# The grouped projection stages of a one-core transformer kernel, spread over four engines

## The reference, cut to what matters

```python
x = x + _L3_attn_ref(_layernorm(x, axis=-1), ...)

def _L3_attn_ref(hidden, ...):                 # rmsnorm eps 1e-6, 16 query heads and 4 key heads of 8
    x = hidden
    x = x + global_latent_attn(rmsnorm(x, norm1_w), g_wq, g_kv_down, g_k_up, g_v_up, g_wo)
    x = x + local_gqa_attn(rmsnorm(x, norm2_w), l_wq, l_wk, l_wv, l_wo)
    return x

def global_latent_attn(x, wq, w_kv_down, w_k_up, w_v_up, wo):
    q = split_heads(x @ wq, H)
    latent = x @ w_kv_down                     # 128 -> 32
    k, v = split_heads(latent @ w_k_up, KVH), split_heads(latent @ w_v_up, KVH)
    q, k = (rope(q, BASE_G), rope(k, BASE_G))
    q, k = (qk_norm(q), qk_norm(k))            # each head of 8 divided by its root mean square
    ...                                        # causal softmax attention, then @ wo
```

## Time and profile before

| | us |
|---|---|
| median of 3 runs (2051.41 to 2062.16) | 2055.13 |
| the profiled execution, its own time | 2044.32 |
| span in that profile, first to last instruction | 2042.2 |
| PE busy in the span | 1736.4 (85%) |
| DVE, ACT, POOL busy | 988.2, 798.6, 288.6 |
| mean granted clock of TensorE | 0.898 |

### The profile page before, as it was taken

The page is one execution under the profiler, slowest core; times in us unless marked ns, Lnnn a source line. Parts: engine busy times, 40 slices in busy tenths (PEclk is TensorE's granted clock), DMA queues, the critical chain, the costliest instruction groups (busy, mean ns, idle before and its releaser), DMA issues. The chain is left out here.

```text
span 2042.2 us, 25586 instructions
## 1 busy us (share of the span) xinstructions
PE 1736.4 (85%) x8894; PEld 926.0 (45%) x8894; DVE 988.2 (48%) x2360; ACT 798.6 (39%) x1283; POOL 288.6 (14%) x439
## 2 busy tenths in 40 slices
PE   7688975699997996996799988996599964988998
PEld 2334653344443663443444445664423332554665
DVE  5755338688782334002620053455733457664444
ACT  5364222267665332221232231221478844553221
POOL 1103320222322431001100030002000010012000
PEclk9898998599998998999799989997589975588999
DMA  3623112201103100000000006550201003103553
GB/s 78 245 62 131 53 41 64 70 25 48 31 20 125 51 22 27 0 0 0 1 0 0 0 24 140 123 115 1 82 28 32 16 1 98 59 24 77 115 120 87
DMA packets 52621, 114.16 MB, mean 56 GB/s; under 512 B 8307, under 2 KB 34547, under 8 KB 47703
## 3 DMA queue, kind: packets, MB, share of 16 engines
q1 hardware_dynamic: 50032, 107.55, 19.1%
q0 software_dynamic: 2432, 5.00, 0.7%
q10 hardware_dynamic: 39, 0.07, 0.0%
HBM read 86.14 MB, written 19.96 MB: 52 GB/s over the span
## 5 line engine op out<-in xcount | busy, mean ns | idle before, releaser
L925 PE MATMUL psum<-f_h,w 128*128 128x512 f32 (+1 forms) x512 | 223.4, 594 | 8.6 <-ACT f_h L896 6.2
L1678 DVE TENSOR_REDUCE a_most<-psum 128x1 f32<-128x512 f32 (+3 forms) x304 | 182.3, 656 | 44.1 <-PE psum L1528 33.1
L1640 ACT ACTIVATE a_probs<-psum 128x512 f32<-128x512 f32 (+1 forms) x304 | 155.7, 577 | 98.6 <-PE psum L1558 97.9
L2443 ACT ACTIVATE t_silu<-psum 128x512 f32<-128x512 f32 x136 | 81.2, 597 | 273.4 <-PE psum L2501 272.4
L2518 PEld LDWEIGHTS psum<-t_slot,t_hid 128*128 128x128 f32 x1024 | 134.8, 194 | 73.6 <-issue 54.3
L925 PEld LDWEIGHTS psum<-f_h,w 128*128 128x128 f32 x512 | 96.0, 190 | 131.7 <-issue 118.9
L2613 DVE TENSOR_TENSOR t_prod<-t_silu,psum 128x512 f32<-128x512 f32 x112 | 77.1, 688 | 155.0 <-ACT t_silu L2443 150.0
L2518 PE MATMUL psum<-t_slot,t_hid 128*128 128x128 f32 x1024 | 137.0, 279 | 16.5 <-DVE t_hid L2604 16.5
L1916 ACT ACTIVATE ga_probs<-psum 128x1024 f32<-128x1024 f32 (+2 forms) x160 | 138.7, 949 | 31.3 <-PE psum L1832 31.1
L2501 PE MATMUL psum<-xnT,t_slot 128*128 128x512 f32 x256 | 133.4, 603 | 3.1 <-ACT t_silu L2443 3.1
L2506 PE MATMUL psum<-xnT,t_slot 128*128 128x512 f32 x256 | 131.9, 597 | 0.0
(11 more groups left out here) (364 smaller groups left out, 2887.9 us busy)
## 6 DMA issues: line engine op xcount, KB each, us to landing
t_spread<-factors SPq DMA_DIRECT2D x64, 512.0 KB, 6.5
m_experts<-experts_dram SPq DMA_DIRECT2D x14, 768.0 KB, 10.8
c_halves<-xnT SPq DMA_DIRECT2D x48, 128.0 KB, 2.3
t_slot<-experts_dram SPq DMA_DIRECT2D x32, 192.0 KB, 5.3
a_qs<-scratch_q SPq DMA_DIRECT2D x48, 96.0 KB
a_ks<-scratch_k SPq DMA_DIRECT2D x24, 192.0 KB
ga_qs<-scratch_q SPq DMA_DIRECT2D x48, 96.0 KB
la_qs<-scratch_q SPq DMA_DIRECT2D x48, 96.0 KB
```

Of the source, the lines that this page charges most:

```text
L925: ins = pe.matmul(core.psum[:, HID[n % 2], :], w(name, i * HT + j), src, start=(i == 0), stop=(i == HT - 1))
L1640: act.activation(probs[:, (n * BLOCKS + b) % PROBS, h0:h0 + heads, 0:wide], src, ACT.Exp, scale=SCALE).then_inc(probs_ready, 1)
L1678: v.tensor_reduce(most[:, row, h0:h0 + heads, qt % KPH], src, AX.X, ALU.max).then_inc(max_read, 1)
```

## The change

norm_stage("n2_") is gone; the g stage does the layer norm itself, by chunks (LayerNorm on DVE and POOL). The rms norm's mean square now comes from ACT (Square with an accumulator, a tile at a time), its root from POOL, its scaling from ACT. Cosine and sine stand spread out in a table that POOL writes at the start of the stage, and DVE does one product of 320 columns for a tile. POOL sums the two halves, takes the mean, the Newton step and the second subtraction of the parts; ACT takes the squares; DVE keeps the first product, the sum over each head, the reciprocal, the first subtraction and the scaling. PE does project(c+1), then turn(c). ACT takes the root of chunk c ahead of the copies of chunk c-1's first part; a chunk's third part is copied by ACT in turn c+2 of the loop. SP's list (sync_all) has the same order as before. Allocations of tiles and semaphores, removed lines (they are in the listing above) and bodies that stay the same are left out:

```diff
--- before.py
+++ after.py
@@ -171,13 +171,16 @@
...
+        for c in range(NC):
+            self.pool_chunk(g, c)
+    def pool_chunk(self, g, c):
...
@@ -1137,9 +1140,12 @@
...
+    def done(self, sp, c, i):
+        sp.wait_ge(self.part_ready, self.parted(c, self.PARTS - 1, i))
     def sync(self, sp, c, i):
...
-        sp.wait_ge(self.part_ready, self.parted(c, self.PARTS - 1, i))
+        self.done(sp, c, i)
...
@@ -1160,6 +1166,54 @@
...
+class PartedSplit(Split):
+    def __init__(self, core, ctx, tag, rows, stacks):
+        super().__init__(core, ctx, tag, rows, stacks)
+        self.first = [core.sb(ctx, f"{tag}first{i}", [r, 2, CH]) for i, r in enumerate(rows)]
+        self.second = [core.sb(ctx, f"{tag}second{i}", [r, CH]) for i, r in enumerate(rows)]
...
+    def copy(self, act, c, p, sources):
+        for i in range(2):
+            if p == 0:
+                act.wait_ge(self.heads_pe, 2 * c + i + 1)
+                if c >= 2:
+                    act.wait_ge(self.spilled[i][c % 2], 16 * (c // 2))
+                source = sources[i]
+            elif p == 1:
+                act.wait_ge(self.rest_ready, 2 * c + i + 1)
+                source = self.first[i][:, c % 2, :]
+            else:
+                act.wait_ge(self.second_ready, 2 * c + i + 1)
+                source = self.second[i][:, :]
+            act.activation(self.parts[i][:, p, c % 2, :], source, ACT.Copy).then_inc(self.part_done[p], 1)
+    def first_rest(self, v, c, sources):
+        for i in range(2):
+            v.wait_ge(self.part_done[0], 2 * c + i + 1)
+            if c >= 2:
+                v.wait_ge(self.part_done[1], 2 * (c - 2) + i + 1)
+                v.wait_ge(self.second_ready, 2 * (c - 2) + i + 1)
+            v.tensor_tensor(self.first[i][:, c % 2, :], sources[i], self.parts[i][:, 0, c % 2, :], ALU.subtract).then_inc(self.rest_ready, 1)
+    def second_rest(self, g, c):
+        for i in range(2):
+            g.wait_ge(self.part_done[1], 2 * c + i + 1)
+            if c:
+                g.wait_ge(self.part_done[2], 2 * (c - 1) + i + 1)
+            g.tensor_tensor(self.second[i][:, :], self.first[i][:, c % 2, :], self.parts[i][:, 1, c % 2, :], ALU.subtract).then_inc(self.second_ready, 1)
+    def read(self, pe, c):
+        pe.wait_ge(self.rest_ready, 2 * c + 2)
+    def done(self, sp, c, i):
+        for p in range(self.PARTS):
+            sp.wait_ge(self.part_done[p], 2 * c + i + 1)
...
@@ -2628,15 +2682,14 @@
...
+    FULL = kind == "g"
...
@@ -2644,154 +2697,284 @@
...
-        ln = Norm(core, ctx, tag, core.xn, xr, rms=True, eps=EPS)
-        sp_ = Split(core, ctx, tag, (P, VW), stacks)
+        sp_ = PartedSplit(core, ctx, tag, (P, VW), stacks)
+        first = LayerNorm(core, ctx, tag + "x_") if FULL else None
...
+        table = core.sb(ctx, tag + "table", [P, T // P, 2, HD * GROUP])
+        turned_by = core.sb(ctx, tag + "turned_by", [P, TPC, 2 * QK])
...
+        QKV_BANK, T_BANK, LN_BANK = (0, 1, 2, 3), (4, 5), (6, 7)
...
+        @block.gpsimd
+        def _(g):
+            s = Steps(g, pool_step)
+            g.wait_ge(w5_in, 16)
+            for r, name in enumerate(("cos", "sin")):
+                a, n = L3_COLS[kind + name]
+                src = w5[:, a:a + n].rearrange("p (t d) -> p t d", d=HD).unsqueeze(3).broadcast_to([P, T // P, HD, GROUP])
+                g.tensor_copy(table[:, :, r, :].rearrange("p t (d h) -> p t d h", h=GROUP), src).then_inc(table_ready, 1)
+            def rms(c):
+                g.wait_ge(power_ready, TPC * (c + 1))
+                r = core.rstd[:, TPC * c:TPC * (c + 1)]
+                s.chain(g.tensor_scalar(r, power[:, TPC * c:TPC * (c + 1)], 1.0 / D, EPS, ALU.mult, ALU.add))
+                g.tensor_tensor(r, r, core.mhalf[:, TPC * c:TPC * (c + 1)], ALU.pow).then_inc(rms_ready, 1)
+            def add(c):
+                g.wait_ge(turned_ready, TPC * (c + 1))
+                if c >= 2:
+                    g.wait_ge(sp_.heads_pe, 2 * (c - 1))
+                g.tensor_tensor(heads[:, c % 2, :, :], turned_by[:, :, 0:QK], turned_by[:, :, QK:2 * QK], ALU.add).then_inc(summed, 1)
+            def newton(c):
+                g.wait_ge(inverse_ready, c + 1)
+                s.chain(g.tensor_tensor(slope[:, :, :], root[:, :, :], root[:, :, :], ALU.mult))
+                s.chain(g.tensor_tensor(slope[:, :, :], slope[:, :, :], mean[:, :, :], ALU.mult))
+                s.chain(g.tensor_scalar(slope[:, :, :], slope[:, :, :], -0.5, 1.5, ALU.mult, ALU.add))
+                if c:
+                    g.wait_ge(heads_ready, c)
+                g.tensor_tensor(scale[:, :, :], root[:, :, :], slope[:, :, :], ALU.mult).then_inc(scale_ready, 1)
+            if FULL:
+                first.pool_chunk(g, 0)
+            for c in range(NC):
+                if FULL and c + 1 < NC:
+                    first.pool_chunk(g, c + 1)
+                rms(c)
+            add(0)
+            for c in range(NC):
+                g.wait_ge(reduced, c + 1)
+                if c:
+                    g.wait_ge(scale_ready, c)
+                g.tensor_scalar(mean[:, :, :], total[:, :, :], 1.0 / HD, EPS, ALU.mult, ALU.add).then_inc(mean_ready, 1)
+                g.wait_ge(mean_ready, c + 1)
+                newton(c)
+                if c >= 2:
+                    sp_.second_rest(g, c - 2)
+                if c + 1 < NC:
+                    add(c + 1)
+            sp_.second_rest(g, NC - 2)
+            sp_.second_rest(g, NC - 1)
...
+            def turn_x(c):
+                if c >= 2:
+                    pe.wait_ge(xnT_ready, c - 1)
+                for t in range(TPC):
+                    pe.wait_ge(xr_ready, TPC * c + t + 1)
+                    ins = pe.transpose(core.psum[:, LN_BANK[c % 2], t * P:(t + 1) * P], xr[:, TPC * c + t, :], core.c("ident"))
+                ins.then_inc(xr_turned, 1)
+            def latents(c):
+                pe.wait_ge(xnT_ready, c + 1)
+                if c >= 2:
+                    pe.wait_ge(latent_ready, c - 1)
+                pe.matmul(core.psum[0:LATENT, LAT_BANK[c % 2], :], w("g_down"), core.xnT[:, c * CH:(c + 1) * CH],
+                          start=True, stop=True).then_inc(latent_pe, 1)
+            def project(c):
+                pe.wait_ge(xnT_ready, c + 1)
+                if FULL:
+                    pe.wait_ge(latent_ready, c + 1)
+                for t in range(TPC * c, TPC * (c + 1)):
+                    if c:
+                        pe.wait_ge(turned_ready, t - TPC + 1)
+                        pe.wait_ge(v_ready, t - TPC + 1)
...
+                    ins.then_inc(qkv_pe, 1)
...
+            turn_x(0)
+            turn_x(1)
+            if FULL:
+                latents(0)
+            turn_x(2)
+            if FULL:
+                latents(1)
+            project(0)
+            turn_x(3)
+            if FULL:
+                latents(2)
+                latents(3)
+            for c in range(NC):
+                if c + 1 < NC:
+                    project(c + 1)
+                turn(c)
...
+            def power_of(c):
+                for t in range(TPC * c, TPC * (c + 1)):
+                    if FULL:
+                        act.wait_ge(first.xn_ready, t + 1)
+                    if t:
+                        act.wait_ge(power_ready, t)
+                    act.activation(squares[:, :], core.xn[:, t, :], ACT.Square, accum_out=power[:, t:t + 1]).then_inc(power_ready, 1)
+            def normalise(c):
+                act.wait_ge(rms_ready, c + 1)
+                for t in range(TPC * c, TPC * (c + 1)):
+                    act.activation(xr[:, t, :], core.xn[:, t, :], ACT.Copy, scale=core.rstd[:, t:t + 1]).then_inc(xr_ready, 1)
+            def turned_x(c):
+                act.wait_ge(xr_turned, c + 1)
+                act.activation(core.xnT[:, c * CH:(c + 1) * CH], core.psum[:, LN_BANK[c % 2], :], ACT.Copy,
+                               scale=w("norm1" if FULL else "norm2")).then_inc(xnT_ready, 1)
+            def latents(c):
+                act.wait_ge(latent_pe, c + 1)
+                act.activation(latent[:, c * CH:(c + 1) * CH], core.psum[0:LATENT, LAT_BANK[c % 2], :], ACT.Copy).then_inc(latent_ready, 1)
+            def values(c):
+                for t in range(TPC * c, TPC * (c + 1)):
+                    act.wait_ge(turned_ready, t + 1)
+                    act.activation(v_all[:, t, :], core.psum[:, QKV_BANK[t % TPC], 2 * QK:2 * QK + VW], ACT.Copy).then_inc(v_ready, 1)
+            def squares_of(c):
+                act.wait_ge(summed, c + 1)
+                if c:
+                    act.wait_ge(reduced, c)
+                act.activation(square[:, :, :], heads[:, c % 2, :, :], ACT.Square).then_inc(squared, 1)
+            power_of(0)
+            power_of(1)
+            normalise(0)
+            turned_x(0)
+            power_of(2)
+            normalise(1)
+            turned_x(1)
+            if FULL:
+                latents(0)
+            power_of(3)
+            normalise(2)
```

(56 more changed lines are left out.)

141 lines of the change are left out of this document (43 added, 98 removed).

## The result

| | median us | lowest to highest | executions |
|---|---|---|---|
| before | 2055.34 | 2038.98 to 2063.61 | 20 |
| after | 2074.86 | 2056.74 to 2084.68 | 20 |

The ratio is 1.0094, with a 95% interval of 1.0065 to 1.0122: the changed kernel is slower by about 19.5 us. The profiled execution of after took 2065.63 (span 2063.8), 21.3 more than that of before.

A forecast was written before the change was run, and what follows sets the result against it. VectorE was taken to bound the chunk loop and SyncE's list the stage ends; preparation, chunks, spill and list gave stages of 96.3 and 77.5 us, +15.5 and +12.8, together +28, so 2083 on the 2055.1 median; range 2055 to 2099.

The forecast's parts named there:

- step 1: First stage's preparation with the norm moved in: sum over heads of chunk 0 at 36.7 us, against 34.2 before.
- step 2: Second stage's preparation, where no norm is saved: sum over heads of chunk 0 at 22.5 us, against 17.8 before.
- step 3: Chunk loop: scaling to scaling 5.1 or 5.5 us plus the projection; chunk 3's sum starts at 64.1 and 45.3.
- step 4: From chunk 3's sum over heads to chunk 1's first spill: 6.9 us, so spills at 71.0 and 52.2.
- The sentence on which the forecast rested: Stage ends, set by SyncE's list: a stage can't end earlier than 24.7 us after the spill of chunk 1.
- P: TensorE's projection of one chunk: 8.8 or 4.8 us in the first stage, 3.5 in the second.
- Contention: GpSimd in the way of VectorE's scalings 1 and 2: 0.5 and 0.9 us in each stage, 2.8 in all.
- (a): Full-clock projections, GpSimd at its cheap end: stages near 82 to 85 and 72 to 76, +9 to +19; chance 0.17.
- (b): Half clock throughout, projection 8.8 twice, GpSimd terms at their dear end: 2095 to 2101 us; chance 0.08.
- (c): SyncE doesn't set the end: stages end 1.9 us behind the last part, 81 and 63, no change; chance 0.08.
- (d): Shorter SyncE load issues and full-clock projections: stages end at 70.3 and 61.2 us, -14, so 2041; chance 0.06.
- (e): VectorE's chain still takes near 10.9 us a chunk, making the stage ends later still; chance 0.03.

The follow-up runs named there:

- a_late: Changed kernel with load(1) and load(2) moved from SyncE's list in the two projection stages to the head of its attention-stage list; ratio to before 1.0019.
- a_early: Changed kernel with the parts of chunk c-1 finished and copied in turn c, SyncE's list unchanged; 2051.21 us in one execution.
- a_scale: Changed kernel with VectorE's first subtraction of chunk c-1 and scaling of chunk c ahead of the products of chunk c+1; 2104.4 us in one execution.
- a_warm190: Changed kernel with 190 unused identity transposes on TensorE behind the last head transposes of each grouped projection stage; 2090.84 us in one execution.
- a_same: Changed kernel, unaltered, profiled once more; 2059.46 us in its execution.
- b_same: Kernel before, unaltered, profiled once more; 2036.17 us in its execution.
- b_idle: Kernel before with five small transfers, each waited for, at the end of SyncE's list in the first grouped projection stage; 2073.43 us in one execution.

## Why the prediction was right, and where it was wrong

| term | predicted | measured |
|---|---|---|
| step 1: sum over heads of chunk 0, first stage | 36.7 | 30.3 |
| step 2: the same, second stage | 22.5 | 19.5 |
| step 3: from there to chunk 3's sum | 27.4, 22.8 | 33.8, 24.7 |
| step 4: to chunk 1's spill | 6.9 | 6.4, 6.5 |
| SyncE's list behind it | 25.3 | 25.5, 25.7 |
| both stages against before | +28.3 | +26.8 |
| attention stages | 0 | -8.2 (the first) |

**What held.** The sentence on which the forecast rested: SyncE's list, read off as 24.7 and a late part of 0.6, measured 25.5 and 25.7. a_late, a_early and a_scale moved it from three sides. Of the signs named for it these are there: the spill at 70.5 and 50.7 (71 and 52), no gap in SyncE's queue, the last part 14.9 us ahead of the last spill, and VectorE waiting for TensorE's projections. One is not: the sum over heads of chunk 0 is later than before in the second stage alone (19.5 against 17.8); in the first it is 3.9 earlier. The prices of operations that the trace of before lacks held too: the product of 320 columns 0.49, GpSimd's addition of 640 columns 1.53 (1.55), its 80 columns 0.32 to 0.35 (0.37), ScalarE's square 0.74 (0.70).

**Steps 1 and 2, too long by 6.4 and 3.0.** I took the cold price for project(0), 8.8, and for the latents behind it; the granted clock rose after project(0)'s first tile and was 1.00 from 1426 to 1436. From after, TensorE and VectorE:

```profile
1424.26 0.80 PE L2831 MATMUL psum<-w,xnT 128*128 128x128 f32 x2
...
1426.17 0.49 PE L2831 MATMUL psum<-w,xnT 128*128 128x128 f32 x2
...
1427.50 0.49 DVE L2959 TENSOR_TENSOR gp_turned_by<-psum,gp_table 128x320 f32<-128x320 f32 x1 [0.66 <-PE psum L2834]
...
1430.43 1.90 PE L2816 MATMUL psum<-xnT,w 128*32 128x512 f32 x4
```

Matmuls at 0.80 become 0.49, and the four tiles take 5.6: 3.2 of the 6.4. What follows them up to the sum over heads took 4.1 instead of 6.4, 2.3 more, mostly because latents 2 and 3 took 1.90 (the last row) and not 3.6. The cold price itself was right: a_warm190 had the half clock there and paid 8.8. The last 0.9 of the first stage, and 2.0 of the second stage's 3.0, come ahead of project(0), which starts at 20.6 and 13.0 instead of 21.5 and 15. They are ScalarE's squares, 16 of which stand in front of it: I added the two rows to 0.56, but the instructions overlap, and one square starts some 0.49 (first stage) or 0.43 (second) behind the one before it:

```profile
1673.81 0.19 ACT L2877 ACTIVATION_READ_ACCUMULATOR lp_squares<-xn_row 128x1 f32 x1
1674.03 0.31 ACT L2877 ACTIVATE lp_squares<-xn_row 128x128 f32<-128x128 f32 x1
1674.24 0.19 ACT L2877 ACTIVATION_READ_ACCUMULATOR lp_squares<-xn_row 128x1 f32 x1
1674.46 0.31 ACT L2877 ACTIVATE lp_squares<-xn_row 128x128 f32<-128x128 f32 x1
```

**Step 3, too short by 6.4 and 1.9.** In the prediction's own terms, each counted to the end of a scaling:

| term | predicted | measured |
|---|---|---|
| from the sum over heads of chunk 0 to scaling 0 | 5.2, 5.2 | 7.0, 6.5 |
| from there to scaling 1 | 11.9, 8.6 | 13.3, 9.3 |
| from there to scaling 2 | 10.3, 9.0 | 13.3, 8.8 |

The first term was said to have "none of it", no wait for a projection. But the products of chunk 1 stand ahead of scaling 0 in VectorE's list, and in the first stage the fourth of them waited 1.70 for TensorE, whose clock had fallen to 0.50 at 1436. Scaling 0 started at 1440.13, though GpSimd's Newton step had ended at 1438.24. In the second stage it was GpSimd's addition in the way, 1.3. The other terms of the first stage were mis-sized by the clock: it stayed at 0.50 from 1436 to the stage's end. From after, VectorE (the brackets say what it waited for):

```profile
1439.72 0.49 DVE L2959 TENSOR_TENSOR gp_turned_by<-psum,gp_table 128x320 f32<-128x320 f32 x1 [1.70 <-PE psum L2834]
...
1447.09 0.49 DVE L2959 TENSOR_TENSOR gp_turned_by<-psum,gp_table 128x320 f32<-128x320 f32 x1 [0.99 <-PE psum L2834]
1449.29 0.49 DVE L2959 TENSOR_TENSOR gp_turned_by<-psum,gp_table 128x320 f32<-128x320 f32 x1 [1.70 <-PE psum L2834]
1451.48 0.49 DVE L2959 TENSOR_TENSOR gp_turned_by<-psum,gp_table 128x320 f32<-128x320 f32 x1 [1.70 <-PE psum L2834]
```

A tile comes every 2.20 us, the cold price of the earlier trace rows, in chunk 2 and chunk 3 alike: P was 8.8 in both periods, where I had taken 6.8 and 4.8, and the rest of the period was 4.5 instead of 5.1 and 5.5. From chunk 0's sum to chunk 3's the first stage took 33.8 us, against 32.8 in before: there the loop of the chunks got no shorter at all, with less work on VectorE. VectorE waits most for this. From after, the waits of VectorE between 1403 and 1500 (us in total, times, longest us):

```profile
DVE gp_turned_by L2959 <- PE psum L2834: 25.7, 13, 11.0
```

11.0 of it is the wait for the very first tile; the other twelve waits, 14.7 together, stand between tiles. That chunk 3's sum came at 64.1 us exactly as predicted is a coincidence: +6.4 and -6.4 cancel. In the second stage the errors leave 44.2 against 45.3.

**The attention, 8.2 of the miss.** "The attention stages keep their instructions, and both start at the half clock before and, I expect, after" was right in both halves, and the conclusion, nothing, was wrong: what counts is how long TensorE then stays at the half clock. This term had no range. With -8.2 the sum gives 2055.1 + 28.3 - 8.2 = 2075, where 2074.9 was measured; that it fits so closely is luck, since the stages were 1.5 off and the -8.2 is from one pair of traces. The spread of 174 to 185, and that of 81 to 112 in the second attention stage, were nowhere in the trace of before, since one trace shows one value; they should have been charged as bounds of both signs.

**Contention.** Charged at 0.5 and 0.9 for scalings 1 and 2 of each stage, 2.8 in all; measured 0.36 + 0.36 and 0.36 + 1.17, 2.3 in all, and 1.3 more for scaling 0 of the second stage. The size held, its place didn't.

**Rivals.** By the time alone the result doesn't choose: +19.5 lies just under the forecast's +20 to +37 and just above (a)'s +9 to +19. (The ends that (a) names for the stages add up to +8.5 to +15.5 only.) The ends of the stages do choose. (a) needed the full clock: it was there in the second stage, which came out at (a)'s upper end, 76; in the first it was not, and the stage took 96 instead of 82 to 85. (b) had P = 8.8 twice, which came in the first stage, but with a preparation that was 6.4 shorter. (c), (d) and (e) fell: SyncE sets the end, the spill of chunk 1 comes far behind 56.1, and VectorE's work in the chunk did shrink. The period that (e) names, near 10.9, came in the first stage all the same (11.3 on average), set by TensorE's projections.

## What to carry to other kernels

Find what the last instruction of a stage waits for, follow it back in its queue until the queue itself was waiting, and price a change by when it delivers that item: here all work that was taken off VectorE was worth nothing, because the item that SyncE's in-order list wanted first came 16 us later in the first stage and 12.6 in the second. When work is spread over engines to shorten a chain, check that the parts that feed transfers don't move back a turn in the order; issues of DMAs that nobody needs yet belong behind those that end the stage. And a following stage of dense matmuls is not a constant: give the time that it spends at the half clock a range. Before one trace is compared with another, compare the stages that the change doesn't touch.

## What the runs showed of the hardware

**VectorE's scaling and GpSimd's addition exclude each other, in both orders.** Both read two tiles in SBUF. From after:

```profile
1440.13 0.82 DVE L2976 TENSOR_TENSOR gp_heads<-gp_heads,gp_scale 128x640 f32<-128x640 f32 x1
1440.29 2.05 POOL L2768 TENSOR_TENSOR gp_heads<-gp_turned_by 128x640 f32<-128x640 f32 x1 [2.04 <-DVE gp_turned_by L2959]
...
1697.33 1.53 POOL L2768 TENSOR_TENSOR lp_heads<-lp_turned_by 128x640 f32<-128x640 f32 x1
1697.40 2.14 DVE L2976 TENSOR_TENSOR lp_heads<-lp_heads,lp_scale 128x640 f32<-128x640 f32 x1 [0.19 <-POOL lp_scale L2777]
```

The one that starts first takes its usual time (0.82; 1.53), and the later one ends about its own time behind the other's end: VectorE's at 1699.54, 0.68 behind GpSimd's; GpSimd's at 1442.34, 1.39 behind VectorE's. The Trainium skill (SBUF — State Buffer, Who interferes with whom) says that a VectorE instruction with two SBUF inputs contends with a GpSimd instruction that reads SBUF, by an exclusive lock; the rows agree, and a scaling next to an addition can cost 1.3 us. VectorE's first subtraction, with one operand in PSUM, ran beside the same addition at 1452 without a loss (1.27 for two, 1.28 elsewhere; the addition 1.53).

**The time to the full clock.** In the first attention stage, with the same TensorE instructions, the clock stood at its full rate for good 8, 17, 23, 27 or 30 us after the start, though TensorE was busy for nearly all of that time (4.00 of every 4 us in before). After and a_same both had 8, before 23 and b_same 30. Neither 18 us of idle time ahead of it (b_idle) nor being busy at nearly the full clock until 2.8 us before it (a_warm190) accounts for it. In the second attention stage the mean granted clock was between 0.53 (a_scale, 111.6 us) and 0.81 (b_same, 85.6 us), again for the same 976 instructions. The cause is open.
